# Cosine-attention scores of a decoder kernel: one full-array product per head pair against two 64-row products

## What is computed

```
def l2norm(t, eps=1e-12):
    n = jnp.maximum(jnp.linalg.norm(t, axis=-1, keepdims=True), eps)
    return t / n
...
q, k, v = map(split_heads, (q, k, v))          # 16 heads of 64 channels
k = jnp.concatenate([nk, k], axis=2)           # one null key ahead of 64 context keys
v = jnp.concatenate([nv, v], axis=2)
q = l2norm(q) * q_scale
k = l2norm(k) * k_scale
sim = jnp.einsum('bhid,bhjd->bhij', q, k) * 8.0
attn = jax.nn.softmax(sim.astype(jnp.float32), axis=-1)
out = jnp.einsum('bhij,bhjd->bhid', attn, v)
out = out.transpose(0, 2, 1, 3).reshape(b, -1, 1024) @ Wout
return layer_norm(out, g_out)
```

## Time and profile before

| what | value |
|---|---|
| median of three runs | 1374.71 us |
| all three | 1370.11, 1374.71, 1378.59 us |
| span of the profiled execution | 1374.7 us |
| TensorE matmul busy | 1243.7 us, 90% |
| TensorE weight loads busy | 828.6 us, 60% |
| VectorE busy | 1048.2 us, 76% |
| ScalarE busy | 517.7 us, 38% |
| GpSimd busy | 267.8 us, 19% |
| mean granted TensorE clock | 0.963 of full speed |

### The profile page before, as it was taken

One profiled execution on the slowest core, in us unless ns is written; L12 is line 12 of the kernel. 1 busy time (PEld: TensorE's weight loads), 2 busy tenths in 40 slices (PEclk: granted clock), 3 DMA queues, 4 the chain that ended last, 5 costly groups with the idle time before them and its releaser, 6 DMA issues.

```text
span 1374.7 us, 18473 instructions
## 1 busy us (share of the span) xinstructions
PE 1243.7 (90%) x7340; PEld 828.6 (60%) x7340; DVE 1048.2 (76%) x1966; ACT 517.7 (38%) x608; POOL 267.8 (19%) x194
## 2 busy tenths in 40 slices
PE   7899999997999999853779999999999999998976
PEld 4566666665644554321566776767768686766654
DVE  3578899986634789998564787969878797887777
ACT  1244334433534567587013323232322333231421
POOL 0011111112100000033100413204132141413242
PEclk9899999999999999976899999999999999999998
DMA  5001000102582045489322011100211000000000
GB/s 219 16 16 32 31 1 31 32 16 93 150 295 77 31 153 185 167 315 373 107 87 84 31 54 62 54 31 32 63 54 54 32 24 21 27 20 36 1 16 16
DMA packets 47829, 107.86 MB, mean 78 GB/s; under 512 B 10752, under 2 KB 31360, under 8 KB 44288
## 3 DMA queue, kind: packets, MB, share of 16 engines
q1 hardware_dynamic: 43584, 104.59, 21.7%
q10 hardware_dynamic: 4160, 2.10, 0.5%
HBM read 62.64 MB, written 44.04 MB: 78 GB/s over the span
## 4 chain that ended last, share of the span: by engine, by line
PE 74%; DVE 16%; DMA 3%; ACT 3%; issue 2%; POOL 1%; SPq 0%; POOLq 0%; ACTq 0%; DVEq 0%
PE ps L1357 8%; PE ps L1420 7%; PE ps L1236 6%; PE ps L1067 6%; PE ps L1118 4%; PE ps L817 4%; PE ps L1393 3%; PE ps L1302 3%; PE ps L965 2%; PE ps L890 2%; PE ps L1326 2%; PE ps L1337 2%; PE ps L1467 2%; DMA arena<-up_scratch 2%; PE ps L908 2%
## 5 line engine op out<-in xcount | busy, mean ns | idle before, releaser
L1420 PE MATMUL ps<-arena 128*128 128x256 f32 x512 | 120.1, 389 | 5.8 <-ACT arena L1892 5.8
L1357 PE MATMUL ps<-arena 128*128 128x512 f32 x256 | 117.6, 598 | 0.0
L1420 PEld LDWEIGHTS ps<-arena 128*128 128x128 f32 x512 | 98.6, 195 | 27.9 <-ACT arena L1892 9.9
L2535 DVE TENSOR_TENSOR arena<-ps,arena 128x2048 f32<-128x2048 f32 x32 | 73.3, 2292 | 38.1 <-PE ps L1302 37.9
L1938 POOL TENSOR_TENSOR arena<-arena 128x4 f32<-128x4 f32 x44 | 45.5, 1038 | 282.0 <-DVE arena L2124 282.0
L1998 POOL TENSOR_TENSOR arena<-arena 128x16 f32<-128x16 f32 x32 | 92.2, 2916 | 32.5 <-DVE arena L2564 32.5
L1236 PE MATMUL ps<-arena 128*128 128x256 f32 x384 | 88.2, 386 | 5.2 <-DVE arena L2456 5.2
L1067 PE MATMUL ps<-arena 128*128 128x512 f32 x192 | 83.8, 593 | 1.2 <-ACT arena L1620 1.2
L1118 PE MATMUL ps<-arena 128*128 128x512 f32 x192 | 84.4, 594 | 0.0
L1236 PEld LDWEIGHTS ps<-arena 128*128 128x128 f32 x384 | 73.0, 194 | 16.5 <-issue 7.0
L1357 PEld LDWEIGHTS ps<-arena 128*128 128x128 f32 x256 | 46.2, 190 | 48.7 <-issue 45.1
(11 more groups left out here) (311 smaller groups left out, 2651.9 us busy)
## 6 DMA issues: line engine op xcount, KB each, us to landing
v_scratch<-arena SPq DMA_DIRECT2D x7, 1536.0 KB, 12.9
arena<-v_scratch SPq DMA_DIRECT2D x7, 1536.0 KB, 6.8
up_scratch<-arena SPq DMA_DIRECT2D x6, 1536.0 KB, 6.0
arena<-up_scratch SPq DMA_DIRECT2D x6, 1536.0 KB, 12.6
vw_scratch<-arena SPq DMA_DIRECT2D x32, 256.0 KB, 3.8
arena<-x_scratch SPq DMA_DIRECT2D x16, 512.0 KB, 4.7
arena<-vw_scratch SPq DMA_DIRECT2D x8, 1024.0 KB
arena<-x SPq DMA_DIRECT2D x8, 512.0 KB, 5.7
```

The costliest lines, as they stand in the source:

```text
L1357: last = mm(flat(p % 2), w["cos_wq"][:, k, p * P:(p + 1) * P], xt4[:, k], start=k == 0, stop=k == NC - 1)
L1420: last = mm(flat(2)[:, C:2 * C], cos_pt[:, p], cos_vw[:, par, p], start=p == 0, stop=p == NP - 1)
L2535: v.tensor_tensor(met_s[:, n % 2].rearrange("p r t h n -> p (r t h) n"), flat(3, 4).rearrange("p (h n) -> p h n", n=P), w["causal"].unsque ...
```

## The change

The scores of a pair come from two products, one for each head. Each takes the 64 partitions of its head: the 128 query columns as weights and the head's 64 keys as what is streamed. The first heads of the pairs write one bank and the second heads the next one, so both banks hold eight blocks of 64 columns. The zero quarters are gone: `cos_kb` is half as wide, the memset and its event are gone, ScalarE waits for two `pads_cleared` events and SyncE for none, and the keys of a batch come with one DMA of 128 partitions. VectorE reads the scores through views that put the heads back in their order, head r of pair q from bank r. Everything in the arena behind `cos_kb` moves down by 1024 words.

```diff
@@ arena @@
-        cos_kb = ar.take(2, NP, P)
+        cos_kb = ar.take(2, NP, TC)
@@ helpers @@
+        def scores_by_pair(b, t):
+            return flat(score_bank(b, t), 2).rearrange("p (r q k) -> p q r k", r=2, k=TC)
+
+        def by_pair(ap):
+            return ap.rearrange("p (q r) -> p q r", r=2)
@@ cos_load @@
                 if b.first():
-                    sp.wait_ge(ev("pads_cleared"), 1)
                     sp.wait_ge(ev("ck_stored"), 16 * 4)
...
-                for lo, hi in ((0, CD), (CD, P)):
-                    sp.dma_start(cos_kb[lo:hi, par, :, lo:hi], ck_d[lo:hi, :, at])\
-                        .then_inc(moved("cos_k_loaded", par), 16)
+                sp.dma_start(cos_kb[:, par], ck_d[:, :, at]).then_inc(moved("cos_k_loaded", par), 16)
@@ cos_scores @@
-                        pe.wait_ge(moved("cos_k_loaded", par), b.half(32, 32))
+                        pe.wait_ge(moved("cos_k_loaded", par), b.half(16, 16))
...
                     for p in range(NP):
-                        last = mm(flat(score_bank(b, t), 2)[:, p * P:(p + 1) * P], cos_q[:, p, t * P:(t + 1) * P],
-                                  cos_kb[:, par, p], start=True, stop=True)
+                        for r, (lo, hi) in enumerate(((0, CD), (CD, P))):
+                            last = mm(flat(score_bank(b, t) + r)[:, p * TC:(p + 1) * TC],
+                                      cos_q[lo:hi, p, t * P:(t + 1) * P], cos_kb[lo:hi, par, p], start=True, stop=True)
                     last.then_inc(sig("cos_scored", NT).sem, 1)
@@ ScalarE, GpSimd @@
-            act.wait_ge(ev("pads_cleared"), 3)
+            act.wait_ge(ev("pads_cleared"), 2)
...
-            g.memset(cos_kb, 0.0).then_inc(ev("pads_cleared"), 1)
@@ cos_scale @@
-                    v.tensor_tensor(s, flat(score_bank(b, t), 2).rearrange("p (h k) -> p h k", h=H),
-                                    rn.unsqueeze(2).broadcast_to([P, H, TC]), ALU.mult)\
+                    v.tensor_tensor(s.rearrange("p (q r) k -> p q r k", r=2), scores_by_pair(b, t),
+                                    by_pair(rn).unsqueeze(3).broadcast_to([P, NP, 2, TC]), ALU.mult)\
                         .then_inc(sig("cos_scaled", NT).sem, 1)
@@ cos_raw_max @@
-                    link(v.tensor_reduce(cos_mx[:, t % 2], flat(score_bank(b, t), 2).rearrange("p (h k) -> p h k", h=H),
-                                         AX.X, ALU.max))
+                    link(v.tensor_reduce(by_pair(cos_mx[:, t % 2]), scores_by_pair(b, t), AX.X, ALU.max))
```

## The result

| | before | after |
|---|---|---|
| median, runs | 1372.34 us, 12 runs (1368.87 to 1378.59) | 1377.43 us, 12 runs (1373.58 to 1381.79) |
| ratio, 95% interval | | 1.0029 [1.0015, 1.0042] |
| span of the profiled execution | 1374.7 us | 1379.2 us |
| mean granted TensorE clock | 0.963 | 0.961 |
| TensorE matmuls busy | 1243.7 us, x7340 | 1253.0 us, x7852 |

The change costs 0.29%, 2 to 6 us: 4.0 by the ratio, 4.5 between the two profiled spans. 4.9 was forecast, to a total of 1379.6 us. That total was added to a span, and a run's time lies some 1.8 us above its own span (1381.01 against 1379.2 in the profiled run of the changed kernel), while the twelve runs put the kernel before at 1372.34 and not at 1374.71; so the difference is what can be compared. One run of the kernel before, among those made beside e5 to e7, took 1668.23 us at a mean clock of 0.741 and is left out of the ratios.

A forecast was written before the change was run, and what follows sets the result against it. The prediction took TensorE to bound the kernel, with three quarters of the chain of waits on it. Five batches at 4.15, the sixth's 0.49 and the seventh's 0.30 made 4.9 us, added to 1374.7: 1379.6 us, range 1371 to 1386.

The forecast's parts named there:

- The pace of the pairs: TensorE's scores steps: pairs of products start 0.112 us apart, set by the load of 128 weight columns.
- Rival A: Scores steps: pairs go at the matmul's pace, 0.056 us, each step 0.84 us shorter; 1363.7 us in all; chance 0.07.
- Halves side by side: Scores steps: loads to different row halves overlap, so 32 loads take 1.69 us from first to last start, against 1.68.
- rival B: Scores steps: the two halves' loads go one after the other, +1.78 us a step over the forecast; 1421 us; chance 0.08.
- 0.19 us for each change of tiling: TensorE, each border between whole array and tiles: 0.09 + 0.10 = 0.19 us.
- The gain of 0.055 from narrow last columns: End of each scores step: the last pair's columns pass in 0.055 us instead of 0.112, gaining 0.055 a step.
- The four steps by their neighbours: Steady batch's scores steps: first 0.34, second 0.15, third free in slack, fourth 0.34; batch 0.83 us longer.
- Rival C: TensorE's borders: changes of tiling cost nothing or other waits take them up; 1375 us; chance 0.10.
- Split banks and key loads at nothing: VectorE's reads from alternating banks, and the key load with one issue fewer: each counted as 0 us.
- rival D: VectorE pays for the split banks, 0.2 to 1 us in `cos_scale`; up to 1386 us; chance 0.05.
- The last three batches: Sixth to eighth batch: 0.49 us for the sixth's first two scores steps, 0.30 in the seventh, nothing in the eighth.
- the fourth step of the seventh batch: Scores step at 1277.80 us: 0.15 us longer, as VectorE takes over the chain from the step's end.

The follow-up runs named there:

- e5_border: Changed kernel with the first scores step moved behind the third part of met_out: 1375.62 us, one run; steady batch 82.97 us against 83.17.
- e7: Changed kernel with four 64 by 64 tiles and the first scores step behind the third part of met_out: 1368.27 us, ratio 0.9962 to the kernel before.
- e1_wide: Changed kernel with 128 streamed columns instead of 64 in each 64-row product but a step's last pair: 1378.09 us, ratio 1.0042 to the kernel before.
- e6_quads_wide: Changed kernel with four tiles of 64 weight columns, but 128 streamed columns except in a step's last pair: 1376.05 us, one run, batch 82.78 us.
- e2_quads: Changed kernel with each tile's 128 tokens split too, four products of 64 by 64 by 64 per pair: 1369.98 us, ratio 0.9973 to the kernel before.
- e3_in_turn: Changed kernel with the eight products of the first heads, then the eight of the second: 1434.3 us, two runs, ratio 1.0445 to the kernel before.
- e4_loads: Changed kernel with the key buffer's memset, its event and waits, and two key DMAs put back: 1378.85 us, ratio 1.0041 to the kernel before.

## Why the prediction was right

**The pace of the pairs** (0.112, set by the load). Right: 32 loads in 1.86 us, and e1_wide with e6_quads_wide shows it by experiment. Rival A was wrong for this shape; e2_quads shows the shape for which it nearly holds. The Trainium skill (TensorEngine Tiling (Array Packing), Theoretical Speedup) allows up to twice the speed for a contraction of 64 or less. No run shows that with 128 columns of weights; with 64 by 64 tiles the step goes from 1.95 to 1.16 us, a factor of 1.7.

**Halves side by side.** Right; rival B is ruled out by the same 1.86. e3_in_turn shows its mechanism with a price: 1.39 us a step.

**0.19 us for each change of tiling.** Right as a sum: 0.20 in e5_border. Inside it two terms were off and cancelled, which is luck. The gain of 0.055 from narrow last columns does not show: the last matmul takes 0.272, not 0.22, and the step behind starts 0.20 later, as behind any other border. In its place the block is only 0.05 us longer than its pace gives (2.00 - 0.272 against 15 x 0.112), where 0.10 was taken.

**The four steps by their neighbours,** 0.34 + 0.15 + 0.34 and the third free. Right: 0.82 to 0.83 a batch, 4.15 in five, 0.47 for the first two steps of the first batch, and 0.3 off the wait ahead of `cos_turn`. Rival C is dead with it.

**Split banks and key loads at nothing.** Right. e4_loads shows the loads, and the group of `cos_scale` in the changed kernel (count, busy us, mean ns) shows the banks, 1.215 us where it took 1.217, so that rival D has nothing to stand on:

```profile
L2581 DVE TENSOR_TENSOR arena<-ps,arena 128x1024 f32<-128x1024 f32 x32 | 38.9, 1215 | 0.2 <-issue 0.2
```

**The last three batches.** The sixth batch's first two steps lie in the steady part, and the seventh's second step is the +0.14 of e4_loads: both as forecast. Mis-sized is the fourth step of the seventh batch, taken at 0.19 - 0.055 + 0.01 = 0.15 "since VectorE takes over from there with the step's end". The way back to the whole array was left out, and it counts. Before and after:

```profile
1277.63 1.95 PE L1393 MATMUL ps<-arena 128*128 128x128 f32 x16
1279.42 1.04 PE L1407 MATMUL ps<-arena 128*128 128x128 f32 x8
1281.57 3.72 PE L1420 MATMUL ps<-arena 128*128 128x256 f32 x16 [1.11 <-ACT arena L1892]
```

```profile
1283.03 2.00 PE L1397 MATMUL ps<-arena 64*128 64x64 f32 x32
1284.96 1.10 PE L1411 MATMUL ps<-arena 128*128 128x128 f32 x8
1287.17 3.72 PE L1424 MATMUL ps<-arena 128*128 128x256 f32 x16 [1.11 <-ACT arena L1896]
```

The chain goes on over `cos_turn` on TensorE (line 1407, at 1279.58 in the chain before), and VectorE takes over only behind that. From the step to the next `cos_out` it is 4.14 us instead of 3.94. Another 0.10 comes in ahead of the step: it now starts 0.06 us before the `cos_out` block in front of it ends, where it started 0.16 before that. This makes 0.30 in all, twice the 0.15. The steps of the eighth batch add nothing, as forecast: from line 1467 at 1310.45 (1471 at 1316.04) to the eighth `cos_out(0)` it is 23.19 us in both kernels, and in e4_loads.

By these rows the change itself costs 0.47 + 4.15 + 0.14 + 0.30 = 5.1 us where 4.9 stood. The spans differ by 4.5; what is left between the two, by subtraction, is +1.3 in the stretch from the sixth to the seventh `cos_out(0)`, -0.8 in the next and -1.1 in the last. It goes with the clock: the block of 5.41 in the first of them, the blocks of 4.67 and 3.86 in the second, a clock of 0.91 instead of 0.87 in the third. The forecast had no term for it, so part of its nearness to 4.5 and 4.0 is luck.

The windows behind the last reading, from the eighth `cos_out(0)` to the end, before and after:

```profile
1333.64:1374.70 41.06, 25.96 (x112) 20.09 (x112) 32.30 (x92) 7.55 (x10) 11.19 (x16) 0.87 0.04 13
```

```profile
1339.23:1379.20 39.97, 24.90 (x112) 19.32 (x112) 32.27 (x92) 7.54 (x10) 11.16 (x16) 0.91 0.04 14
```

## What to carry to other kernels

Removing products with zeros saved nothing here, where only the streamed side shrank and the load set the pace: ask which of the two, load or stream, sets the distance from one product to the next, and narrow both. Count the borders between whole array and tiles, and between two kinds of tiles, in the order of the steps, and price each from a place in the trace that has one already. A step that is made shorter on the leading engine pays only up to the next wait for another engine, and moving that engine's work to end the wait can open one behind it.

## What the runs showed of the hardware

One 64 by 64 tiling of the array ran four float32 products in the time of one: 64 matmuls in 1.16 us, the sets 0.058 us apart, and their loads 0.135 us each (0.188 for 128 columns). A change between the whole array, 32-column tiles and 64-row tiles cost 0.20 us (e5_border). The time of a launch goes with the clock that is granted. Runs of the kernel before with a mean of 0.967 took 1369.1 to 1373.0 us, those at 0.961 took 1376.9 to 1377.9; the steady batches show 1.00 in either profile, and the falls lie elsewhere, the last of them in the tail, where a block of `cos_out` takes 5.41 or 5.89 us instead of 3.72.
